# The zero fills of the table of rows by expert: issued by SP in the scan stage and not by ACT in the first stage

## The reference, cut to what matters

```python
x = x + _L0_xattn_ref(_layernorm(x), fside, ctx)    # int8-style linears: scales by column and row, rounded
x = x + _L0_ffn_ref(_layernorm(x), lut, gate_idx, up_idx, down_idx)   # weights are lut[idx], 1376 wide
x = x + _L1_xattn_ref(ctx, _layernorm(x), ...)      # convolution, then a selective scan of 16 states
x = x + _L1_ffn_ref(_layernorm(x), gate_w, w_gate, w_up, w_down)      # 32 experts, top 8 of each row
```

```python
slot = jnp.where(pos < C, se * C + pos, E * C)
x_pad = jnp.concatenate([x, jnp.zeros((1, H), x.dtype)], axis=0)
xg = x_pad[t_slot].reshape(E, C, H)
```

## Time and profile before

| | |
|---|---|
| median of 3 runs | 2120.91 us (2116.69 to 2123.33) |
| the profiled execution, its own time | 2115.85 us |
| its span, first to last instruction | 2114.1 us |
| first stage, to the first scan of the next | 0 to 529.9 us |
| scan stage | to about 1210 us |
| busy in the span | PE 1531.1, DVE 1440.6, ACT 905.1, POOL 673.9 us |
| moved by DMA | 455.04 MB, of it 106.06 on ACT's queue, 280.11 on SP's |
| the 16 large fills | 4096 KB each, 20.8 us from issue to landing in the median |
| mean granted TensorE clock | 0.853 of full |

### The profile page before, as it was taken

The page is one execution under the profiler, slowest core; times in us unless marked ns, Lnnn a source line. Parts: engine busy times, 40 slices in busy tenths (PEclk is TensorE's granted clock), DMA queues, the critical chain, the costliest instruction groups (busy, mean ns, idle before and its releaser), DMA issues. The chain is left out here.

```text
span 2114.1 us, 26326 instructions
## 1 busy us (share of the span) xinstructions
PE 1531.1 (72%) x9312; PEld 1303.2 (62%) x9312; DVE 1440.6 (68%) x2096; ACT 905.1 (43%) x1579; POOL 673.9 (32%) x450
## 2 busy tenths in 40 slices
PE   5767787774599699699689442105999999999920
PEld 3444454443499589589679431105888899998820
DVE  6676786864898999999999452003666655558954
ACT  3535555453444544534534140003555666665510
POOL 1010000101544644644554136770000000007876
PEclk9879788977699799799799775557999999999965
DMA  7888798844637338437435045653668666668877
GB/s 222 294 280 299 242 361 306 268 155 146 249 127 293 148 125 296 155 112 277 178 129 176 25 151 203 255 212 128 200 208 287 210 210 210 210 209 312 294 216 232
DMA packets 167496, 455.04 MB, mean 215 GB/s; under 512 B 17328, under 2 KB 19376, under 8 KB 157632
## 3 DMA queue, kind: packets, MB, share of 16 engines
q1 hardware_dynamic: 90880, 280.11, 39.6%
q10 hardware_dynamic: 56000, 106.06, 13.7%
q0 software_dynamic: 20480, 67.13, 9.2%
HBM read 271.83 MB, written 181.40 MB: 214 GB/s over the span
## 5 line engine op out<-in xcount | busy, mean ns | idle before, releaser
L1116 POOL TENSOR_TENSOR mix_st<-mix_Bb,mix_du 128x2048 f32<-128x2048 f32 x64 | 293.4, 4584 | 278.6 <-DVE mix_st L1401 266.5
L1393 DVE TENSOR_TENSOR_SCAN mix_st<-mix_dA,mix_st 128x512 f32<-128x512 f32 x256 | 311.6, 1217 | 42.9 <-POOL mix_st L1116 22.3
L1802 POOL DMA_INDIRECT moe_gat<-x_by_expert,moe_where x128 | 155.6, 1216 | 513.0 <-DMA x_by_expert<-moe_ys 471.1
L1266 ACT ACTIVATE mix_dA<-mix_dt,mix_A 128x512 f32<-128x512 f32 x256 | 177.0, 691 | 285.1 <-DVE mix_st L1393 281.4
L1187 PE MATMUL mix_G<-mix_xThi,mix_wup 128*128 128x256 f32 x1408 | 278.9, 292 | 14.3 <-issue 14.3
L1926 PE MATMUL moe_G<-moe_xhi,moe_whi 128*128 128x288 f32 x768 | 234.5, 305 | 14.0 <-issue 10.3
L1187 PEld LDWEIGHTS mix_G<-mix_xThi,mix_wup 128*128 128x128 f32 x1408 | 232.4, 198 | 17.2 <-issue 15.8
L1926 PE MATMUL moe_G<-moe_xhi,moe_wlo 128*128 128x288 f32 x768 | 228.6, 298 | 9.6 <-issue 9.6
L1926 PE MATMUL moe_G<-moe_xlo,moe_whi 128*128 128x288 f32 x768 | 228.8, 298 | 8.2 <-issue 8.2
L1213 PE MATMUL mix_Y<-mix_ident,mix_st 128*128 128x128 f32 x1024 | 150.3, 297 | 92.1 <-DVE mix_st L1401 92.1
L2275 DVE TENSOR_TENSOR moe_xlo<-moe_T,moe_xhi 128x512 fp32r<-128x512 f32 (+1 forms) x160 | 101.9, 637 | 156.0 <-issue 79.9
(11 more groups left out here) (235 smaller groups left out, 3231.0 us busy)
## 6 DMA issues: line engine op xcount, KB each, us to landing
x_by_expert<-front_zeros ACTq DMA_DIRECT2D x16, 4096.0 KB, 20.8
mix_wup<-w_halves SPq DMA_DIRECT2D x44, 1024.0 KB, 5.5
moe_raw<-in_ew SPq DMA_DIRECT2D x32, 1280.0 KB
moe_xt<-x_by_expert SPq DMA_DIRECT2D x128, 256.0 KB
x_by_expert<-moe_ys ACTq DMA_DIRECT2D x128, 256.0 KB
mix_wdn<-w_halves SPq DMA_DIRECT2D x44, 512.0 KB, 6.3
front_idx<-in_idx SPq DMA_DIRECT2D x44, 384.0 KB, 8.4
w_halves<-front_wst SPq DMA_DIRECT2D x44, 384.0 KB, 7.6
```

The costliest lines, as they stand in the source:

```text
L1116: nc.gpsimd.tensor_tensor(st[:, g % STBUF, :, :], Bb[:, q, :, :], du[:, k % 2, :].unsqueeze(1).to_broadcast([P, NG, S]), ALU.mult).then_in ...
L1266: nc.scalar.activation(dA[:, :], dt[:, k % 2, :], ACT.Exp, scale=A[:, c, m:m + 1]).then_inc(da_ready, 1)
L1393: nc.vector.tensor_tensor_scan(r, dA[:, :], r, 0.0, ALU.mult, ALU.add).then_inc(scanned, 1)
L1802: pool.indirect_dma_start(out=gat[:, q, :], out_offset=None, in_=s["XG"], in_offset=bass.IndirectOffsetOnAxis(ap=where[:, i, k:k + 1], axi ...
```

## The change

The zeros tile moves from the first stage's memory to the scan stage's, POOL makes it there, and SP issues the 17 fills in slots 2, 5, 8, ... 50 of the scan stage, behind the weights of that slot. The first stage's wait for the fills goes; the third stage's stays. The sizes are the same. The semaphore counts of the constants change by one.

```diff
-FILLS_AT = range(4, 4 + 9 * 17, 9)
...
-        zeros = sb("zeros", [P, D], F32)
...
-            sp.wait_ge(filled, 16 * (FILLS + 1))
...
-            nc.gpsimd.memset(zeros[:, :], 0.0).then_inc(pool_made, 1)
...
-                if t in FILLS_AT:
-                    i = FILLS_AT.index(t)
-                    fill(act, s, zeros, i * FILL, FILL if i < FILLS else 1, filled)
...
-def mix_block(nc, d, s):
+def mix_block(nc, d, s, filled):
...
+        zeros = sb("zeros", [P, D], F32)
...
                     load_down(downs)
                     downs += 1
+                if g in FILLS_AT:
+                    if g == FILLS_AT[0]:
+                        sp.wait_ge(pool_made, 5)
+                    i = FILLS_AT.index(g)
+                    fill(sp, s, zeros, i * FILL, FILL if i < FILLS else 1, filled)
                 if l == 10:
...
+            nc.gpsimd.memset(zeros[:, :], 0.0).then_inc(pool_made, 1)
...
+FILLS_AT = range(2, 2 + 3 * (FILLS + 1), 3)
```

More of the change, by code:

```diff
@@ L374, in _ @@
             nc.gpsimd.iota(kcoli[:, :], pattern=[[2, PAIRS]], base=0, channel_multiplier=0).then_inc(pool_made, 1)
-            pool.wait_ge(pool_made, 4)
+            pool.wait_ge(pool_made, 3)
             nc.gpsimd.affine_select(out=ident[:, :], in_=ident[:, :], compare_op=ALU.not_equal, fill=1.0, base=0,
@@ L379, in _ @@
                                     pattern=[[-1, ROWS_H]], channel_multiplier=1).then_inc(pool_made, 1)
-            pool.wait_ge(pool_made, 6)
+            pool.wait_ge(pool_made, 5)
             nc.gpsimd.affine_select(out=ident2[:, :], in_=ident2[:, :], compare_op=ALU.not_equal, fill=1.0, base=-ROWS_H,
@@ L416, in _ @@
         def _(pe):
-            pe.wait_ge(pool_made, 15)
+            pe.wait_ge(pool_made, 14)
             pe.wait_ge(small_in, 16 * 6)
@@ L560, in _ @@
             act.dma_start(dtb[:, :], d["dtb"]).then_inc(small_in, 16)
-            act.wait_ge(pool_made, 15)
+            act.wait_ge(pool_made, 14)
             def normalise(b):
@@ L712, in _ @@
             link = Link(dve, dve_link)
-            dve.wait_ge(pool_made, 15)
+            dve.wait_ge(pool_made, 14)
             def moments(b):
@@ L1149, in _ @@
         def _(pe):
-            pe.wait_ge(pool_made, 5)
+            pe.wait_ge(pool_made, 6)
             def rows_transposes(b):
@@ L1249, in _ @@
             act.wait_ge(const_in, 32)
-            act.wait_ge(pool_made, 5)
+            act.wait_ge(pool_made, 6)
             nc.scalar.activation(A[:, :, :], A[:, :, :], ACT.Exp).then_inc(a_made, 1)
@@ L1359, in _ @@
         def _(dve):
-            dve.wait_ge(pool_made, 5)
+            dve.wait_ge(pool_made, 6)
             link = Link(dve, dve_link)
@@ L2436, in build @@
         front_block(nc, d, s, filled)
-        mix_block(nc, d, s)
+        mix_block(nc, d, s, filled)
         moe_block(nc, d, s, out, filled)
```

## The result

| | median of the runs | ratio to before, 95% interval | profiled span |
|---|---|---|---|
| before | 2120.51 us (4 runs) | | 2114.1 us |
| after | 2155.31 us (4 runs, 2150.07 to 2155.36) | 1.0162 [1.0144, 1.0179] | 2153.5 us |

The change costs 34.8 us. The direction was forecast, and the time lies in the range of 2117 to 2161, but the forecast was +13.6: the loss is two and a half times that.

A forecast was written before the change was run, and what follows sets the result against it. PE was taken to bound the scan stage's dense slots; first-stage engines wait for each other. Late loads 12.2 + clock 3.4 - first stage 2 = +13.6 us, so 2134.5 us from the median 2120.91; range 2117 to 2161.

The forecast's parts named there:

- The mechanism: Scan stage: SP's queue is served in issue order, so loads behind a fill come late and PE waits, some 12 us.
- Rival A: Scan stage: loads issued behind a fill share the engines with it, nothing is late, 2119 to 2125 us; chance 0.25.
- The clock term: Scan stage: after a pause PE's clock is partly halved, 1.7 us lost each; two pauses give 3.4 us.
- The first stage, -2: First stage: without the fills' traffic the one-hot compare runs faster, a gain of 2 us, bounds 0 and 6.0.
- Rival B: First stage: really slowed by fill traffic and ACT issues, 12.4 us back, total 2111 us; chance 0.09.
- The three dense fills: Scan slots 8, 26, 44: next up load within 1 us of need, late by 4.1, late by 4.0.
- the rate: Scan stage: SP's loads move at 402 GB/s, 2.6 us for 1024 KB; a fill at 384 GB/s, 10.9 us.
- my upper case: Scan stage: down loads land a microsecond later than summed, added to late cases and plain slots; lateness 14.9 us, not 9.5.
- Ends of batches and columns: Scan slots including 14 and 32: up loads have 14 us or more; slots 29 and 47 cost 0, 3 each uncovered.
- The plain dense fills: Scan slots 8, 11, 23, 41: within 1 us of need, 0.1 in all; slot 38 late by 1.3.
- Rival C: Scan stage: SP held in issues asks late, 2.2 us more per dense fill, batch ends late; 28 more, 2162; chance 0.16.

The follow-up runs named there:

- e1_act: Changed kernel with the fills in the same scan-stage slots but issued by ACT on its own queue: 2012.73 us against 2005.54 for the kernel before.
- e6_both: Changed kernel with all fills also issued by ACT in the first stage, as in the kernel before: 2156.39 us against 2115.69 for the kernel before.
- e5_after: The changed kernel itself, unaltered, run again as control on the second chip: 2158.46 us against 2115.69 for the kernel before.
- e10_only_three: Changed kernel with only the fills of slots 8, 26, 44 in the scan stage, the other fourteen in the first on ACT: 2142.28 us against 2118.17 before.
- e7_late: Changed kernel with each fill behind the B rows, columns and x transfers, directly ahead of the next up load: 2144.1 us against 2115.69 before.
- e3_quarter: Changed kernel with quarter-size fills, one in every scan-stage slot, on SP's queue: 2005.51 us against 2005.54 for the kernel before.
- e8_narrow: Changed kernel with a zeros tile of half the width, 4096 pieces of 1 KB per fill: 2166.16 us against 2115.69 for the kernel before.
- e9_late_three: Changed kernel, fills of slots 8, 26, 44 moved to 3, 19, 36, every fill behind B rows, columns and x transfers: 2123.2 us against 2118.17 before.

## Why the prediction was wrong in size

**Right.** The mechanism: a load issued behind a fill in SP's queue comes after it, and PE waits for `mix_wup`, longest behind the fills that I named, those of slots 26 and 44. Rival A (the engines are shared) falls for one queue and holds for two (e1_act): an up load lands 14.9 us after its issue behind a fill, and 0.86 and 0.76 MB go side by side in e1_act. The Trainium skill (DMA: Bandwidth & Descriptors, Queues, rings and completion order) has ring order inside one queue and turns between queues; both traces agree. The clock term: forecast 1.7 us a pause, found 1.7 and 1.9.

**The first stage, -2.** Nothing came back. The compare's mean is 1048 ns as before, and e6_both, with the fills in the first stage, is no slower than e5_after. The slow compares have another cause, not looked for. Rival B falls.

**The three dense fills, the term that was mis-sized.** The prediction had 0 to 1 us for slot 8, 4.1 to 5.1 for slot 26, 4.0 to 5.0 for slot 44, and 3.4 for the clock: 11.5 to 14.5. The steps of after make 21.1, those of e10_only_three 23.8. The failed step is the rate: I took 402 GB/s, from the start of the stage, for every load. The trace of before has other rates in the very slots of the sum, for an up load and three columns alone in the queue:

```profile
613.00:616.00 3.00, 3.00 (x28) 3.00 (x27) 2.97 (x5) 1.04 (x2) 2.57 (x1) 1.00 0.86 277
616.00:619.00 3.00, 3.00 (x17) 2.56 (x16) 2.97 (x5) 1.68 (x4) 2.05 (x1) 1.00 0.91 298
```

and after, around the fill of slot 8:

```profile
616.00:619.00 3.00, 3.00 (x21) 2.71 (x21) 2.97 (x5) 1.49 (x4) 2.99 (x1) 1.00 0.92 297
619.00:622.00 3.00, 3.00 (x23) 2.81 (x22) 3.00 (x5) 1.44 (x3) 0.00 (x0) 1.00 1.05 410
622.00:630.00 8.00, 8.00 (x61) 7.56 (x60) 7.23 (x10) 4.10 (x9) 4.61 (x1) 1.00 1.06 397
630.00:633.00 3.00, 3.00 (x27) 2.96 (x26) 3.00 (x5) 0.93 (x2) 0.00 (x0) 1.00 0.88 207
633.00:637.00 4.00, 1.02 (x10) 0.78 (x8) 3.29 (x5) 1.07 (x2) 3.22 (x1) 1.00 0.89 331
```

The fill itself runs at 397 to 410 GB/s, a little better than the 384 of the earlier trace rows. The loads ahead of it and the columns behind it do not. (The queue of the stage's start, at 402, held columns too, so it is not the kind of load alone.) At slot 8 the next up load was issued at 623.76 and landed at 637.5, 24.6 us after T = 612.90; 402 GB/s would have given 20.9, and PE was ready at 634.0. The 3.5 us late are nearly all of the 24.6 - 20.9 = 3.7. Of these, 0.6 had come about when the fill landed (T+16.9 against T+16.3) and 3.0 behind it. At slot 44 the load landed at T+28.1 where I had T+24.8, and there the fill was already 2.3 us late. At slot 26, where only large transfers stand behind the fill, T+26.8 against T+25.4: there my upper case, with the microsecond more, was nearly right, 5.1 + 1.7 against a step of 7.0.

The trace of before could have given more than the rate did. In it the columns of slot 9 landed 8.1 us after T, those of slot 45 12.5 us and the load of x of slot 26 13.9 us after it. With 10.9 us for the fill and 2.6 for the up load added, an estimate from these rows, the up loads land at T+21.6, T+26.0 and T+27.4. With the columns ahead of the fill, in e7_late, they landed at T+22.4, T+26.8 and T+26.8. Most of what is missing in after, at T+24.6 and T+28.1, is what columns lose behind a fill, 1.3 to 2.7 us by e7_late. Why they lose it stays open.

**Ends of batches and columns, costed at 0.** The prediction gave slots 14 and 32 no cost, on the ground that up loads have 14 us or more. Of B rows it spoke only behind the fills of slots 29 and 47, with 3 us each if the cover were gone, and behind those nothing over 1 us came. For slots 14 and 32 it asked for the up loads only. POOL's B rows and du columns also stand behind these fills. SP of after, from the fill of slot 32 on:

```profile
872.85 4.26 SPq L65 DMA_DIRECT2D x_by_expert<-mix_zeros  x1
877.15 14.75 SPq L1009 DMA_DIRECT2D mix_Cb<-bc_rows  x1
891.95 0.84 SPq L989 DMA_DIRECT2D mix_dt<-dt_store  x1
892.84 0.89 SPq L992 DMA_DIRECT2D mix_du<-du_store  x1
```

The C rows behind the fill take 14.75 us to issue, du goes out at 892.84 and lands 13.6 us later, and POOL, idle for 6.95 us, starts with it at 906.5. The trace has steps of 2.8 and 4.0 at these two places, and e7_late, which puts them ahead of the fill, takes both away. With slot 8's columns this is the 11 us of steps that e7_late recovers.

**The plain dense fills, 1.4 to 4.8 us** (slots 8, 11, 23 and 41 with slot 38): 6.9 us measured without slot 8. Each has PE waits of 0.9 to 1.6. They fit as barely as the prediction said, and miss by one microsecond instead of making it by one.

**Rival C, SP held in its issues.** Its sign in the trace is there: issues of 6.8 to 14.8 us behind fills, where I had counted 0.6. Its reasoning (2.2 us of start-up more for each dense fill, since SP asks late) is not borne out. In after the next up load is issued at 623.76, while the fill lands at 629.8, so its start-up is still hidden, and e3_quarter holds SP as much and loses nothing. Twice the pieces (e8_narrow) cost 7.7 us more, but there too the load was asked for before the fill had landed. Its time, 2162, was nearer than mine in part by luck: 17.6 of its 28 us were for that start-up. What it had right is that ends of batches come late.

The sum in the terms of the profiled executions, 39.4 us: first stage +1.2, the three fills 21.1, ends of batches 6.8, plain fills 6.9, other slots 0.5 in all, third stage 2.9. The last is no effect that can be held to the change: e9_late_three's third stage is 1.3 us shorter than before, e10_only_three's 4.4 longer, with the same bytes. That the fill of slot 44 lands another 2 us later than its bytes at 264 and 405 GB/s account for, by my estimate, stays open.

## What to carry to other kernels

A mean DMA rate of half the peak does not mean that a bulk transfer fits: it fits if it is smaller than the slack of the first load that is queued behind it, so cut it into transfers of that size and spread them, or give it a queue of its own (here +34.8 us became 0 with quarters and +0.3% on ACT's queue). List every load that stands behind the bulk transfer in its queue, each with the engine that needs it, and not only those of the engine that bounds the stage. Take the rate of each from a window in which that kind of load ran or, better, take from the trace when the last of them lands and add the bulk transfer to that; small loads behind it can still lose a few microseconds more.

## What the runs showed of the hardware

- An issue behind a fill holds the issuing engine, and longer with more pieces: 6.8 us behind a fill of 2048 pieces of 2 KB, 10.8 us behind one of 4096 pieces of 1 KB, with the same bytes and nearly the same landing (16.4 and 16.8 us). With quarter fills in every slot no issue of SP took over 6.6 us.
- The same loads take longer behind a fill than ahead of it: with three columns of 256 KB ahead of the fill, the next up load landed 2.7 us earlier, at the same bytes (slot 8 of e5_after and e7_late).
- Loads of 256 KB to 1 MB by themselves ran at 277 to 298 GB/s and at 207 GB/s behind a fill, the fill at 397 to 410. The Trainium skill (DMA: Bandwidth & Descriptors, Specifications) has about 358 GB/s as one core's share of HBM; these traces go over it for whole fills, with one core at work.
- The Trainium skill says (same page, Issuing engines are not separate DMA queues) that initiating DMAs on several engines "will only save the time on the sequencer". Here it did more: the same fills in the same slots, on ACT's queue instead of SP's, gave back 32 of the 36.5 us by which the scan stage ended later, since loads no longer stood behind them.
- A transfer of 4 MB beside the loads of the first stage, on its own queue, cost that stage nothing that shows, even with the DMA engines 0.89 to 0.90 busy: it ended at 528.5 us with the fills (e6_both) and at 530.3 without (e5_after).
